# Mamba's opening split in two: the first four tiles' step sizes and splits are made in the FFN block ahead, the other twelve tiles' follow

## The chip, the core and the metric

The kernel runs on one NeuronCore of a Trainium2 chip. A core has a matrix engine (TensorE, PE in the profile; its weight loads are shown as PEld), a vector engine (VectorE, DVE), an activation engine (ScalarE, ACT), a general engine (GpSimd, POOL) and a queue that issues transfers (SyncE, SP). Each engine works through its own list of instructions in order; semaphores make one wait for another. Matrix results land in PSUM banks, everything else lies in SBUF. The metric is the time of one execution in microseconds (us); lower is better. The time before is 738.0 us, the median of 3 runs (737.44 to 738.93).

## What is computed

Six stages run over 8 sequences of 256 tokens with 128 channels, which are 16 tiles of 128 tokens: a mixture-of-experts FFN, an RWKV block, the same FFN again, a second kind of FFN, a Mamba-2 block, and the second FFN again. The change lies at the seam between the fourth stage and the fifth. Of the Mamba block this matters (N is 16 heads, chunks have 64 tokens):

```python
def mamba2_forward(x, W_in, W_dt, b_dt, W_B, W_C, W_out, A_log):
    xz = x @ W_in.T
    x_in, z = (xz[..., :d], xz[..., d:])
    dt = jax.nn.softplus(x @ W_dt.T + b_dt)
    A = -jnp.exp(A_log)[None, None, :] * dt
    B = (x @ W_B.T).reshape(b, L, h, n)
    C = (x @ W_C.T).reshape(b, L, h, n)
    X = x_in.reshape(b, L, h, p) * dt[..., None]
    Y, new_state = ssd_minimal(X, A, B, C, CHUNK)   # decays exp(cumulated A)
    y = Y.reshape(b, L, d) * jax.nn.silu(z)
    return (y @ W_out.T, new_state)
```

`dt` are the step sizes and `A` the decays, 16 numbers for each token; the decays have to be cumulated along the tokens before the chunks can be worked on.

## The kernel before, in words

**The FFN stream.** `ffn_stream` works in blocks of 4 tiles (512 tokens). The two FFN stages ahead of Mamba are one stream of 8 blocks; the last, block 7, has 12 units p = 0 to 11, two shared ones, eight experts, two shared ones. The order is written out by hand: at unit p, PE makes the two up projections of unit p + 4 (into `ps_a`, `ps_b`, 6 matmuls of 512 columns) and the down projection of unit p (`ps_acc`, 3 matmuls); ACT takes the SiLU of unit p + 4 and rounds unit p + 2 (`hhi`); DVE multiplies for unit p + 4 (`gated`) and takes the remainder of unit p + 2 (`hlo`); POOL weighs the experts. Since a product of 32-bit numbers is made of three passes over rounded and remaining parts (`three_pass`, L98 to L100), nearly every operand has a `hi` and a `lo`.

**What the stream already does for Mamba.** With `heads` set it also normalises and turns the first 12 tiles of Mamba's input: `measure` (L508, L512), POOL's `scale`, `normal` (L520, writes `norm_xn`), `turn_x` (L269, PE transposes into `ps_t`), `high_x` (L389) and `low_x` (L527). Block 10 of this count, which is tiles 8 to 11, is the last: in block 7 DVE normalises it at p = 8, PE turns it at p = 9, ahead of the down projections 10 and 11, ACT and DVE split it at p = 10. Then come `take_out` (L411), `turn_out` (L311) and `add_out` (L559), and a barrier of all engines.

**The opening of `mamba_phase`.** On PE: `steps(0, 12)` (36 matmuls, each with 16 moving columns and 128 columns of weights, tile by tile against `w["dt"]`, into `mb_pyt`), `project(0)` and `project(1)` (input projections, 6 matmuls of 256 columns for two tiles, into the two banks `mb_c`), `turn` (L1864, tiles 12 to 15, which are normalised only here), `project(2)`, `project(3)`, `steps(12, 16)`, `project(4)` to `project(7)`, `cumulate(0)` (L1800: 8 matmuls against the triangle `le` for tiles 0 to 3), `begin_piece(0)`, the sums over all decays (L1907), `begin_piece(1)` to `(3)` (B and C of sequence 0, 12 matmuls of 256 columns each), then the sections. A section is one sequence: four groups of heads, each with decays (L1768), products of B and C (L1793), outputs (L1816) and a piece of the next sequence's B and C.

On ACT: the projections' copies `take_in(k)` (L1975, L1976, which free the bank for `project(k + 2)`), softplus of all 16 tiles at once (Exp L1993, Ln L1995), `take_sums(0)` (L1984), Exp of the sums (`ee`, L2001), the copies `take_bc` (L1929). Exp and Ln need different function tables, so an `ACT_TABLE_LOAD` stands between them.

On DVE: the statistics of the last four tiles, five masks from the identity (`row_masks`, L2027 to L2032), `normed` (L2162), `low_x` (L2168), the triangles' rounded copies (L2178 to L2180), then one chain over 16 tiles (128x256): bias and `-|u|` (L2182, L2185), `dt` (L2187), `dA` (L2189), the split of dA on a grid (`split_sums`, L2038 to L2047: `grid`, `cut`, `cuthi`, `cutlo`), the first four tiles widened to 128 columns (L2049, L2052), the decays' hi and lo (L2191, L2193), `row_parts(0)` (L2063, L2069, L2070), the other twelve tiles' widening (L2057). POOL makes the norm's factors, clears `xp` and `xd`, makes the triangles, and then the first sequence's ranges and inputs.

## Time and profile before

| what | value |
|---|---|
| median of 3 runs | 738.0 us (737.44 to 738.93) |
| the profiled execution | 742.08 us, its span 740.0 us |
| PE busy in the span | 688.9 us (93%) |
| DVE, ACT, POOL busy | 567.0, 415.2, 321.4 us (77%, 56%, 43%) |
| last FFN block's first seam rows to the barrier | 414.9 to 421.7 us |
| Mamba's opening on PE | 421.7 to 454.4 us |
| Mamba's sections on PE | 454.4 to about 618 us |

The span runs from the first instruction to the last of one profiled execution, 2.1 us shorter than that execution's own time and itself 4.1 us over the median of the unprofiled runs. Timeline rows give the start in us from the span's beginning, the length, the engine, the line of the kernel, the operation, what is written from what, and in brackets how long the engine had been idle and who released it. Matmuls are pipelined: their lengths overlap, so the distance between starts is what one costs. The granted clock of TensorE is given as a share of full speed: 1.00 is its 2.4 GHz level, 0.50 its 1.2 GHz level.

### The profile page before, as it was taken

How to read it: one execution, taken by the hardware profiler on the slowest of the kernel's cores; microseconds unless marked ns; L12 is line 12 of the kernel's file. 1: busy time of each engine (PE TensorE's matmuls, PEld its weight loads, DVE VectorE, ACT ScalarE, POOL GpSimd, SP SyncE). 2: the span in 40 equal slices, each digit the busy share in tenths (PEclk: the TensorE clock that was granted, in tenths of full speed). 3: DMA queues.
4: the chain of work that ended last, by engine and by line, in shares of the span. 5: the costliest groups of instructions: out<-in, count | busy, mean ns of one | idle time of the engine just before them, and what ended most of it. 6: DMA issues, size and time to landing. Idle time of an engine off the chain costs nothing. (4 is left out here: it accounts for less than half of the span.)

```text
span 740.0 us, 12506 instructions
## 1 busy us (share of the span) xinstructions
PE 688.9 (93%) x4132; PEld 517.6 (70%) x4132; DVE 567.0 (77%) x1293; ACT 415.2 (56%) x751; POOL 321.4 (43%) x404
## 2 busy tenths in 40 slices
PE   6899989697879999999999778999999997999997
PEld 5677764543457777777778677777777775777785
DVE  5788987899968878987989734566666674889774
ACT  4556775885235555556656446565555553555553
POOL 2658872201217766465668315211413200546463
PEclk9999998999999999999999879999999998999999
DMA  6636510000004232222223000000000000323141
GB/s 169 192 104 181 169 57 1 0 1 1 1 30 143 71 103 96 78 66 80 85 67 106 1 0 1 2 1 2 2 1 1 0 1 1 103 71 121 54 125 43
DMA packets 34329, 43.16 MB, mean 58 GB/s; under 512 B 5216, under 2 KB 17504, under 8 KB 34272
## 3 DMA queue, kind: packets, MB, share of 16 engines
q1 hardware_dynamic: 34272, 42.46, 18.5%
q8 instruction: 29, 0.48, 0.3%
q14 instruction: 28, 0.23, 0.1%
HBM read 41.13 MB, written 1.31 MB: 57 GB/s over the span
## 5 line engine op out<-in xcount | busy, mean ns | idle before, releaser
L677 POOL TENSOR_TENSOR p_prod<-p_p,p_gate_row 128x512 f32<-128x512 f32 x128 | 201.9, 1588 | 110.8 <-DVE p_p L494 64.2
L376 ACT ACTIVATE p_sil<-p_ps_a 128x512 f32<-128x512 f32 x176 | 105.1, 597 | 133.7 <-PE p_ps_a L100 130.2
L499 DVE TENSOR_TENSOR p_hlo<-p_prod,p_hhi 128x512 fp32r<-128x512 f32 x176 | 149.8, 853 | 0.3 <-ACT p_hhi L385 0.2
L494 DVE TENSOR_TENSOR p_p<-p_sil,p_ps_b 128x512 f32<-128x512 f32 x128 | 87.2, 681 | 53.1 <-ACT p_sil L376 39.6
L385 ACT CAST p_hhi<-p_prod 128x512 fp32r<-128x512 f32 x176 | 107.8, 614 | 22.5 <-POOL p_prod L677 22.3
L98 PE MATMUL p_ps_a<-xt_hi,w_uphi 128*128 128x512 f32 x176 | 74.7, 424 | 0.0
L98 PE MATMUL p_ps_acc<-p_hhi,w_downhi 128*128 128x512 f32 x176 | 72.2, 410 | 2.6 <-DVE p_hlo L499 2.5
L98 PE MATMUL p_ps_b<-xt_hi,w_uphi 128*128 128x512 f32 x176 | 71.3, 405 | 1.1 <-DVE p_prod L494 1.1
L100 PE MATMUL p_ps_b<-xt_hi,w_uplo 128*128 128x512 f32 x176 | 70.7, 402 | 0.0
L100 PE MATMUL p_ps_a<-xt_hi,w_uplo 128*128 128x512 f32 x176 | 70.4, 400 | 0.0
L99 PE MATMUL p_ps_acc<-p_hlo,w_downhi 128*128 128x512 f32 x176 | 70.4, 400 | 0.0
L100 PE MATMUL p_ps_acc<-p_hhi,w_downlo 128*128 128x512 f32 x176 | 70.3, 400 | 0.0
L99 PE MATMUL p_ps_a<-xt_lo,w_uphi 128*128 128x512 f32 x176 | 70.2, 399 | 0.0
L99 PE MATMUL p_ps_b<-xt_lo,w_uphi 128*128 128x512 f32 x176 | 70.2, 399 | 0.0
L2078 DVE TENSOR_TENSOR mb_sm<-mb_sm,mb_c 128x512 f32<-128x512 f32 x64 | 43.7, 687 | 27.3 <-ACT mb_off L1951 21.4
L1793 PE MATMUL mb_c<-mb_bc 64*128 64x128 f32 (+1 forms) x512 | 58.9, 349 | 1.3 <-ACT mb_bc L1929 1.3
L1929 ACT COPY mb_bc<-mb_c 128x1024 f32<-128x1024 f32 x32 | 32.4, 1013 | 45.8 <-PE mb_c L100 45.8
L2085 DVE SCALAR_TENSOR_TENSOR mb_sm<-mb_d,mb_later 128x512 f32<-128x512 f32 x64 | 41.2, 685 | 20.7 <-PE mb_d L1768 20.5
L1793 PEld LDWEIGHTS mb_c<-mb_bc 64*128 64x128 f32 x512 | 38.9, 186 | 20.7 <-issue 16.0
L1948 ACT ACTIVATE mb_sm<-mb_sm 128x512 f32<-128x512 f32 x64 | 40.4, 632 | 16.9 <-DVE mb_sm L2085 16.1
L2233 POOL TENSOR_TENSOR w_downhi<-mb_widehi,mb_own 128x512 fp32r<-128x512 f32 x8 | 9.0, 1129 | 94.1 <-DVE norm_moments L2104 46.9
L98 PEld LDWEIGHTS p_ps_b<-xt_hi,w_uphi 128*128 128x128 f32 x176 | 33.5, 190 | 12.1 <-DVE p_p L494 2.3
(345 smaller groups left out, 1452.9 us busy)
## 6 DMA issues: line engine op xcount, KB each, us to landing
p_gate_row<-gate_rows SPq DMA_DIRECT2D x128, 256.0 KB, 3.3
w_rawbuf<-in_L_ffn_fc_w_dram SPq DMA_DIRECT2D x3, 512.0 KB, 6.5
w_rawbuf<-in_L_ffn_w_dram SPq DMA_DIRECT2D x3, 512.0 KB, 6.3
out_dram<-x SPq DMA_DIRECT2D x4, 256.0 KB, 3.7
w_rawbuf<-in_L_ffn_shared_w_dram SPq DMA_DIRECT2D x3, 256.0 KB, 5.7
x<-in_L_attn_x_dram SPq DMA_DIRECT2D x2, 256.0 KB, 3.7
x<-in_L_attn_x_dram SPq DMA_DIRECT2D x1, 512.0 KB, 8.8
mb_xraw<-in_L_attn_W_B_dram SPq DMA_DIRECT2D x1, 512.0 KB, 4.5
```

Of the source, the lines that this page charges most:

```text
L98: pe.matmul(out, weights[0], moving[0], start=start, stop=False)
L99: pe.matmul(out, weights[0], moving[1], start=False, stop=False)
L100: return pe.matmul(out, weights[1], moving[0], start=False, stop=stop)
L376: nc.scalar.activation(sil[:, u % 2], ps_a[:, u % 2], ACT.Silu).then_inc(c["sil"].sem, 1)
L385: nc.scalar.copy(hhi[:, u % R], prod[:, u % R]).then_inc(c["hhi"].sem, 1)
L494: nc.vector.tensor_tensor(dst, sil[:, u % 2], ps_b[:, u % 2], ALU.mult).then_inc(c["p1"].sem, 1)
L499: nc.vector.tensor_tensor(hlo[:, u % R], prod[:, u % R], hhi[:, u % R].bitcast(F32), ALU.subtract).then_inc(c["hlo"].sem, 1)
L677: G.tensor_tensor(prod[:, u % R], p1[:, u % 2], gate_row[:, e % ROWS], ALU.mult).then_inc(c["prod"].sem, 1)
L1793: last = pe.matmul(half(q, t, more)[:, k, 0:SEQ - t * P], bc[h][state, r, j, bass.ts(t, P)], bc[h][state, 2 + r, j, t * P:SEQ], start=True ...
L1948: A(sm[q % 2][t][:], sm[q % 2][t][:], ACT.Exp).then_inc(c["m_E"].sem, 1)
L2078: V.tensor_tensor(sm[q % 2][t][:], sm[q % 2][t][:], half(q, t, more)[:, :, 0:P], ALU.mult).then_inc(c["m_read"].sem, 1)
L2085: V.scalar_tensor_tensor(out=sm[q % 2][t][:], in0=ps_d[t][:], scalar=0.0, in1=later[:].unsqueeze(1).broadcast_to([P, 4, P]), op0=ALU.min, ...
```

## The change

A new class `MambaHead` holds the step sizes' tiles and work, in parts: part 0 is tiles 0 to 3 (the first two sequences), part 1 the other twelve. Part 0 is done inside FFN block 7:

- PE, after down projection 1: `steps` for four tiles, 12 matmuls into the idle logits bank `ps_l`.
- DVE: the triangles' copies in block 6 at p = 9; `biased` at p = 3, `row_masks` at p = 7, `step_sizes` and `split_sums` at p = 10 of block 7.
- ACT at p = 9: Exp of `a_log` and of part 0, a table load ahead of them, a second table load and Ln.
- POOL in block 6 at p = 8: the triangles.

In Mamba's opening PE begins with `project(0)`, `project(1)`, then `cumulate(0)`, `turn`, `project(2)`, `project(3)`, all `steps` of tiles 4 to 15 (36 matmuls), the sums of the first two sequences, `project(4)` to `project(7)`, and four pieces in a row. DVE widens, splits and makes `row_parts(0)` before `low_x`; the chain of part 1 (128x192) follows. ACT takes the sums' Exp in three parts. The sums of the other six sequences, the widening of the twelve tiles and the copies for them move into the first section; `cumulate(1)` with its copy and `row_parts(1)` move from that section's second group of heads to its fourth.

The names with `mb_` in the rows below are the tiles named above; `mb_stage` holds `u` and then `dt`, `mb_na` first `-|u|` and then `dA`. Semaphores (`r_...`) keep the names of an earlier stage.

DVE in block 7, from p = 7 on, before:

```order
L494 TENSOR_TENSOR p_prod<-p_sil,p_ps_b 128x512 [waits s_hhi,s_hlo,s_b,s_sil]
L499 TENSOR_TENSOR p_hlo<-p_prod,p_hhi 128x512 [waits s_hhi] x2
L527 TENSOR_TENSOR xt_lo<-p_ps_t,xt_hi 128x512 [waits s_xhi]
L520 SCALAR_TENSOR_TENSOR norm_xn<-x,norm_moments,norm_rstd 128x128 [waits s_xt,s_rstd,s_moments]
L520 SCALAR_TENSOR_TENSOR norm_xn<-x,norm_moments,norm_rstd 128x128 x3
L499 TENSOR_TENSOR p_hlo<-p_prod,p_hhi 128x512 [waits s_hhi]
```
and now:

```order
L505 TENSOR_TENSOR p_prod<-p_sil,p_ps_b 128x512 [waits s_hhi,s_hlo,s_b,s_sil]
L510 TENSOR_TENSOR p_hlo<-p_prod,p_hhi 128x512 [waits s_hhi]
L1709 TENSOR_REDUCE mb_odd<-ident 128x1
L1710 TENSOR_REDUCE mb_even<-ident 128x1
L1711 TENSOR_REDUCE mb_minus_odd<-ident 128x1
L1712 TENSOR_REDUCE mb_minus_low<-ident 128x1
L1714 TENSOR_REDUCE mb_own<-ident 128x4
L510 TENSOR_TENSOR p_hlo<-p_prod,p_hhi 128x512 [waits s_hhi]
L538 TENSOR_TENSOR xt_lo<-p_ps_t,xt_hi 128x512 [waits s_xhi]
L531 SCALAR_TENSOR_TENSOR norm_xn<-x,norm_moments,norm_rstd 128x128 [waits s_xt,s_rstd,s_moments]
```
Five reductions (the masks) now stand between two remainders of block 7, ahead of `norm_xn`, on which PE's turn waits.

DVE at the end of block 7, before:

```order
L499 TENSOR_TENSOR p_hlo<-p_prod,p_hhi 128x512 [waits s_hhi]
L527 TENSOR_TENSOR xt_lo<-p_ps_t,xt_hi 128x512 [waits s_xhi]
L559 SCALAR_TENSOR_TENSOR x<-p_ps_o,x 128x512 [waits s_ot]
L190 UNCONDITIONAL_BRANCH
L2020 UNCONDITIONAL_BRANCH [waits barrier_Pool_Activation_PE_DVE_SP_release]
```
and now:

```order
L510 TENSOR_TENSOR p_hlo<-p_prod,p_hhi 128x512 [waits s_hhi]
L538 TENSOR_TENSOR xt_lo<-p_ps_t,xt_hi 128x512 [waits s_xhi]
L1662 SCALAR_TENSOR_TENSOR mb_stage<-mb_stage,mb_na 128x64 [waits r_ln]
L1664 SCALAR_TENSOR_TENSOR mb_na<-mb_stage,mb_expa 128x64 [waits r_g2]
L1675 TENSOR_SCALAR mb_grid<-mb_na 128x64 [waits r_low2]
L1677 TENSOR_SCALAR mb_cut<-mb_grid 128x64 [waits r_p]
L1679 SCALAR_TENSOR_TENSOR mb_cut<-mb_na,mb_cut 128x64 [waits r_p]
L1682 CAST mb_cuthi<-mb_cut 128x2x64 [waits r_p]
L1684 TENSOR_TENSOR mb_cutlo<-mb_cut,mb_cuthi 128x2x64 [waits r_x2]
L570 SCALAR_TENSOR_TENSOR x<-p_ps_o,x 128x512 [waits s_ot]
L190 UNCONDITIONAL_BRANCH
```
Seven dependent operations on the first four tiles now stand between `low_x` and the block's `add_out`.

ACT in the opening around softplus, before (after the copies of `project(3)`):

```order
L1993 ACTIVATE mb_na<-mb_na 128x256 [waits r_d]
L1995 ACT_TABLE_LOAD
L1995 ACTIVATE mb_na<-mb_na 128x256 [waits r_S]
L1975 COPY mb_xraw<-mb_c 128x256 [waits r_g]
L1976 ACTIVATE mb_zs<-mb_c 128x256
```
and now (from the same point):

```order
L2107 ACT_TABLE_LOAD
L2107 ACTIVATE mb_ee<-mb_y 128x2x16 [waits r_ev]
L2094 COPY mb_xraw<-mb_c 128x256 [waits r_g]
L2095 ACTIVATE mb_zs<-mb_c 128x256
L2094 COPY mb_xraw<-mb_c 128x256 [waits r_g]
L2095 ACTIVATE mb_zs<-mb_c 128x256
L1654 ACTIVATE mb_na<-mb_na 128x192 [waits r_d]
L1656 ACT_TABLE_LOAD
L1656 ACTIVATE mb_na<-mb_na 128x192 [waits r_S]
```
The Exp of the first sums, with its table load, now stands ahead of the copies of projections 4 and 5, softplus behind them; the copies of 6 and 7, another table load and Exp, and the four B and C copies follow.

The diff, cut to its core:

```diff
 ffn_stream, PE
+                    if heads and (n, p) == (BLOCKS - 1, 1):
+                        pe.wait_ge(c["lgs"].sem, c["lgs"].at(BLOCKS))
+                        pe.wait_ge(c["xlo"].sem, c["xlo"].at(BLOCKS + 1))
+                        pe.wait_ge(c["raw_lo"].sem, c["raw_lo"].at(2))
+                        heads.steps(pe, 0, BT, by_tile(ps_l))
 ffn_stream, ACT
+                    if heads and (n, p) == (BLOCKS - 1, 9):
+                        heads.softplus(act, 0, 0, BT)
 ffn_stream, DVE
+                        if p == 3:
+                            dve.wait_ge(c["raw_lo"].sem, c["raw_lo"].at(len(splits)))
+                            heads.biased(dve, 0, 0, BT, by_tile(ps_l))
+                        if p == 7:
+                            heads.row_masks(dve)
                         if p == 10:
                             low_x(BLOCKS + 2)
+                            heads.step_sizes(dve, 0, 0, BT)
+                            heads.split_sums(dve, 0, 0, BT)
+                    if heads and (n, p) == (BLOCKS - 2, 9):
+                        heads.masks(dve)
 ffn_stream, POOL
+                    if heads and (n, p) == (BLOCKS - 2, 8):
+                        heads.triangles(pool)
 MambaHead
+    def softplus(self, act, part, a, b):
+        act.wait_ge(c["m_na"].sem, c["m_na"].at(part + 1))
+        if part == 0:
+            A(self.exp_a[:], self.vec["a_log"][:], ACT.Exp)
+        A(some, some, ACT.Exp).then_inc(c["m_ex"].sem, 1)
+        act.wait_ge(c["m_ex"].sem, c["m_ex"].at(part + 1))
+        A(some, some, ACT.Ln, bias=1.0).then_inc(c["m_ln"].sem, 1)
...
 mamba_phase, PE
-            steps(0, 3 * BT)
             project(0)
             project(1)
+            pe.wait_ge(c["m_first"].sem, c["m_first"].at(1))
+            cumulate(0, sums_of[0])
             turn()
             project(2)
             project(3)
             pe.wait_ge(c["m_xl"].sem, c["m_xl"].at(1))
-            steps(3 * BT, TILES).then_inc(c["m_pu"].sem, 1)
+            head.steps(pe, BT, TILES, ps_u)
+            sums(0, 0, 2)
             for k in range(4, 8):
                 project(k)
-            pe.wait_ge(c["m_first"].sem, c["m_first"].at(1))
-            cumulate(0, sums_of[0])
-            begin_piece(0)
-            pe.wait_ge(c["m_dl"].sem, c["m_dl"].at(1))
...
-            begin_piece(1)
-            begin_piece(2)
-            begin_piece(3)
+            for k in range(4):
+                begin_piece(k)
 mamba_phase, ACT
             take_in(0)
             take_in(1)
+            take_sums(0)
             take_x()
             take_in(2)
             take_in(3)
...
+            take_ends(0, 0, 1)
+            take_in(4)
+            take_in(5)
+            head.softplus(act, 1, BT, TILES)
+            take_in(6)
+            take_in(7)
+            take_ends(0, 1, 2)
+            for k in range(4):
+                take_bc(0, 0, k, ps_c[k % 2])
 mamba_phase, DVE
             measured_last()
-            row_masks()
+            widen_first()
             normed()
+            split_decays(0, 0, BT)
+            row_parts(0, sums_of[0])
             low_x()
...
+            head.biased(dve, 1, BT, TILES, ps_u)
+            head.step_sizes(dve, 1, BT, TILES)
+            head.split_sums(dve, 1, BT, TILES)
+            split_decays(1, BT, TILES)
```

## Rows read from the trace of the kernel before

**Rows 1.** Engines by stretch: busy us, instructions, granted clock share (PEclk), DMA.

```profile
core 0: us, PE busy (x) PEld busy (x) DVE busy (x) ACT busy (x) POOL busy (x), PEclk, DMA share, GB/s
400.00:414.90 14.90, 14.73 (x66) 11.63 (x65) 14.07 (x28) 8.49 (x16) 11.26 (x9) 1.00 0.14 47
414.90:421.70 6.80, 3.17 (x16) 1.89 (x16) 4.28 (x13) 1.82 (x3) 0.00 (x0) 1.00 0.00 0
421.70:429.40 7.70, 7.68 (x37) 7.70 (x37) 2.60 (x16) 0.85 (x2) 4.87 (x10) 0.50 0.01 3
429.40:435.40 6.00, 6.00 (x29) 6.00 (x30) 1.10 (x4) 2.56 (x7) 0.00 (x0) 0.50 0.00 0
435.50:436.70 1.20, 1.20 (x13) 1.20 (x13) 0.00 (x0) 0.66 (x2) 0.00 (x0) 1.00 0.00 0
435.40:445.50 10.10, 6.12 (x50) 5.71 (x50) 5.27 (x15) 5.50 (x14) 0.00 (x0) 1.00 0.00 0
445.50:449.00 3.50, 3.50 (x19) 3.50 (x18) 2.69 (x5) 1.90 (x3) 1.32 (x1) 0.52 0.02 5
449.20:452.80 3.60, 3.60 (x31) 3.51 (x30) 0.00 (x0) 3.58 (x6) 3.52 (x13) 1.00 0.00 0
474.50:600.00 125.50, 124.43 (x1377) 94.45 (x1376) 84.74 (x169) 72.55 (x118) 29.08 (x91) 1.00 0.01 1
```

**Rows 2.** Timeline, DVE, last FFN block: start, length, operation, idle before, releaser.

```profile
406.17 0.69 DVE L494 TENSOR_TENSOR p_p<-p_sil,p_ps_b 128x512 f32<-128x512 f32 x1 [0.59 <-PE p_ps_b L100]
...
413.65 1.29 DVE L499 TENSOR_TENSOR p_hlo<-p_prod,p_hhi 128x512 fp32r<-128x512 f32 x2
...
417.95 0.69 DVE L527 TENSOR_TENSOR xt_lo<-p_ps_t,xt_hi 128x512 fp32r<-128x512 f32 x1 [0.77 <-ACT xt_hi L389]
...
420.08 0.69 DVE L559 SCALAR_TENSOR_TENSOR x<-p_ps_o,x 128x512 f32<-128x512 f32 x1 [1.43 <-PE p_ps_o L311]
```

**Rows 3.** Timeline, PE and ACT, from the last FFN block's end into the opening.

```profile
416.64 0.66 PE L269 MATMUL p_ps_t<-ident,norm_xn 128*128 128x128 f32 x4 [1.29 <-DVE norm_xn L520]
417.34 0.59 ACT L389 CAST xt_hi<-p_ps_t 128x512 fp32r<-128x512 f32 x1 [2.69 <-PE p_ps_t L269]
...
421.72 0.35 PE L98 MATMUL mb_pyt<-w_uphi,xt_hi 128*128 128x16 f32 x1 [1.68 <-PEq L190]
```

**Rows 4.** Timeline, PE, the opening: the turn, a wait for ACT, the first products.

```profile
432.10 1.05 PE L1864 MATMUL mb_y<-ident,mb_sm 128*128 128x128 f32 x4
...
440.55 0.39 PE L98 MATMUL mb_c<-w_uphi,xt_hi 128*128 128x256 f32 x1 [2.19 <-ACT mb_zs L1976]
...
454.43 1.58 PE L1793 MATMUL mb_c<-mb_bc 64*128 64x256 f32 x16 [0.85 <-ACT mb_bc L1929]
```

**Rows 5.** Timeline, DVE, the opening: the five masks, first and last.

```profile
422.29 0.18 DVE L2027 TENSOR_REDUCE mb_odd<-ident 128x1 f32<-128x64 f32 x1
...
422.77 0.37 DVE L2032 TENSOR_REDUCE mb_own<-ident 128x4 f32<-128x128 f32 x1
```

**Rows 6.** Timeline, ACT and DVE, the first sums' copy and the row parts.

```profile
445.19 0.59 ACT L1984 CAST mb_off<-mb_d 128x512 fp32r<-128x512 f32 x1 [2.24 <-PE mb_d L1800]
445.81 0.75 DVE L2063 SCALAR_TENSOR_TENSOR mb_parts<-mb_off,mb_minus_low,mb_d 128x512 fp32r<-128x512 f32 x1 [1.16 <-ACT mb_off L1984]
447.06 0.54 DVE L2070 TENSOR_SCALAR mb_widelo<-mb_parts,mb_minus_odd,mb_even 128x512 fp32r<-128x512 f32 x1
```

**Rows 7.** Timeline, ACT, the opening: softplus, table loads, copies.

```profile
438.24 1.28 ACT L1995 ACT_TABLE_LOAD   x1
439.54 0.42 ACT L1995 ACTIVATE mb_na<-mb_na 128x256 f32<-128x256 f32 x1
439.86 0.35 ACT L1975 COPY mb_xraw<-mb_c 128x256 f32<-128x256 f32 x1
...
440.64 0.41 ACT L1976 ACTIVATE mb_zs<-mb_c 128x256 f32<-128x256 f32 x1
...
447.36 1.01 ACT L1929 COPY mb_bc<-mb_c 128x1024 f32<-128x1024 f32 x1 [1.58 <-PE mb_c L100]
```

More of the change, by code:

```diff
@@ L108, in __init__, with ffn_stream @@
         self.units, self.shared = weights.units, weights.shared
-def ffn_stream(nc, tag, counts, spare, sb, ps, x, xt, consts, kinds, gate_dram, norm, loads=(), splits=(), out_dram=None, entry=None, begun=0, tail=None, heads=False, opening=None):
+def ffn_stream(nc, tag, counts, spare, sb, ps, x, xt, consts, kinds, gate_dram, norm, loads=(), splits=(), out_dram=None, entry=None, begun=0, tail=None, heads=None, opening=None):
     splits = split_jobs(splits)
@@ L1799, in cumulate @@
                     for k in range(2):
-                        last = pe.matmul(bank[:, t], wide[k][:, g * BT + t], consts["le"][:], start=k == 0, stop=k == 1)
+                        last = pe.matmul(bank[:, t], wide[k][:, g * BT + t], head.le[:], start=k == 0, stop=k == 1)
                 last.then_inc(c["m_C"].sem, 1)
@@ L1865, in turn, with sums @@
                 last.then_inc(c["m_t"].sem, 1)
-            def steps(a, b):
-                for t in range(a, b):
-                    last = three_pass(pe, ps_u[:, t], [q[:, bass.ts(t, P)] for q in xt], w["dt"], True, True)
-                return last
+            def sums(part, a, b):
+                pe.wait_ge(c["m_dl"].sem, c["m_dl"].at(part + 1))
+                for t, tri in ((0, head.gt), (1, head.le)):
+                    for k in range(2):
+                        some = dAp[k][:].rearrange("p (m t) h -> p t m h", t=2)[:, t, a:b]
+                        last = pe.matmul(ps_sum[:, t, a:b], tri[:], some, start=k == 0, stop=k == 1)
+                last.then_inc(c["m_sum"].sem, 1)
             def project(k):
```

235 lines of the change are left out of this document (128 added, 107 removed).

## The prediction

> **What bounds the kernel now.** I read the table of engines by stretch first. In the FFN block ahead of the seam PE is busy 14.73 of 14.9 us, in the sections behind it 124.43 of 125.5 us [rows 1]: there only PE's work counts. Between the two lie 6.8 us of the block's tail, with PE busy 3.17, and the opening. I count the opening from PE's first matmul at 421.72 [rows 3] to the first products of B and C at 454.43 [rows 4], 32.7 us; behind that point the old list and the new one hold nearly the same work. What the change is worth is this length, plus what it adds ahead of the barrier.
>
> Three things are to be seen in the opening. First, the 36 step matmuls take all of 421.7 to 429.4, at a granted clock of 0.50, the 1.2 GHz level (7.7 us over 36, 0.213 each), before any projection starts. Secondly, the clock comes up to 2.4 GHz only at 435.4, after 6.0 us of projections and a turn; then a step matmul costs 0.11 us (1.2 us; of 13 counted two are cut off at the edges) and one of 256 columns 0.12 (3.6 us, 31 counted) [rows 1]. Thirdly, PE stands still for copies that are queued behind softplus on ACT (2.19 us before 440.55, rows 4), and it falls to 0.52 once more for 3.5 us at 445.5 [rows 1].
>
> **The FFN block ahead (dearer).** PE gets 12 step matmuls at p = 1. It runs at 1.00 without a gap there, so they cost 12 x 0.11 = 1.3 us. The logits bank, the turned tiles and `w["dt"]` are ready long before. DVE waited 0.59 us for PE at 406.17 [rows 2], so it moves along by the whole 1.3; the two small operations of `biased` fit into that wait.
>
> The five masks at p = 7 run from 422.29 to 423.14 in the opening today, 0.85 us [rows 5]. In their new place DVE has no idle time until `norm_xn`, and PE waits 1.29 us for just that [rows 2, 3]: +0.85.
>
> Behind `low_x` come seven dependent operations of 64 to 128 columns. Five masks in 0.85 us, and 0.18 for one of 64 columns, bound one at 0.17 to 0.37 with its wait [rows 5]; I take 0.25, near the small one plus a semaphore, so 1.75 us (1.2 to 2.6). They start 1.3 + 0.85 later than `low_x` ends today (418.64), at 420.8, and end at 422.5; `add_out` would come at 420.08 + 2.15 = 422.23 [rows 2]. So +0.3 (0 to 1.1).
>
> ACT's softplus of part 0 costs two table loads of 1.28 us and three small functions (0.42 for 256 columns, so 0.2 to 0.4 each), 3.3 us [rows 7]. ACT is free from 414.65 + 1.3 and is needed for the turned block at 417.34 + 2.15 = 419.49, with 3.5 us between [rows 3]. It hides with 0.2 us to spare; if it doesn't fit, up to 0.5 us falls on the tail. The four triangle operations on POOL and their three copies on DVE (three of the masks' size, 0.5) lie in block 6, ahead of DVE's next wait for PE, and POOL has idle time (11.26 of 14.9 us busy, rows 1): nothing; without that cover 0.5.
>
> Sum ahead of the barrier: 1.3 + 0.85 + 0.3 = **+2.5 us** (2.2 to 3.9).
>
> **The opening (cheaper).** Let t be the time since PE's first matmul. At the 1.2 GHz level: projections 0 and 1, 12 x 0.213 = 2.6; `cumulate(0)`, 8 x 0.213 = 1.7 (its operands are ready at t = 1.5); `turn`, 0.7 (of its 1.05 in rows 4 the last part overlaps what follows); projections 2 and 3 from t = 5.1. The clock came up 6.0 us after the first projection [rows 1]; taken over, they end at 7.0. Meanwhile ACT copies the first sums (0.59), DVE makes `row_parts(0)` (445.81 to 447.60, 1.8 us [rows 6]) and then `low_x` (0.69 [rows 2]): 4.5 + 0.6 + 1.8 + 0.7 = 7.6, so PE waits 0.6 us for it. The 36 step matmuls then cost 36 x 0.11 = 4.0 at 2.4 GHz: done at S = 11.6.
>
> From S on ACT sets the pace. Sums 0.5; table load and small Exp 1.5; two `take_in` 1.2 (439.86 to 441.05, rows 7); softplus 0.4 + 1.3 + 0.4 = 2.1; two `take_in` 1.2; table load and Exp 1.5; four copies of B and C, 1.0 each [rows 7]. The third and the fourth wait for pieces, 12 x 0.12 = 1.45 us each, which wait for the banks: piece 2 starts at S + 9.1, piece 3 ends at S + 12.1, its copy at S + 13.1. DVE's chain for part 1 (nine operations of 192 columns, some 3.5 us) runs beside this and is done before the first section needs it. So the products start at t = 24.8 if the clock stays up.
>
> It will hardly stay up. The long row of 16-column matmuls is just what ran at 1.2 GHz for 7.7 us without bringing the clock up, and a wait of 2.19 us before 440.55 was followed, 5 us later, by 3.5 us at 0.52 [rows 1, 4]. One such stretch costs 3.5 / 2 = 1.7 us of PE's work, of which ACT hides a little: +1.5. That makes t = 26.4 against 32.7: **-6.3 us** (-8 to -4).
>
> **The first section.** `row_parts(1)`, 1.8 us, moves from its second group of heads to the fourth, just ahead of the next section's first operations on DVE, where a second `row_parts` follows. PE may miss 0.3 us (0 to 0.6). The widening copies fall into ACT's and DVE's waits for PE, which has the most to do there (124.4 us of 125.5 against 72.6 and 84.7, rows 1).
>
> **Sum.** 2.5 - 6.3 + 0.3 = -3.5 us. On the profiled execution, 742.1 becomes 738.6; that one lies 4.1 above the median of the runs, and the same difference on 738.0 gives **734.5 us**.
>
> **A rule of the Trainium skill** speaks against the change. The trace shows a table load of 1.28 us at 438.24 and the Ln at 439.54, 0.02 us behind it [rows 7]. "ScalarE: Activation LUTs", section "What ACT_TABLE_LOAD costs", gives about 1.28 us for the load and another 1.38 for a drain, 2.66 in all for each switch. The load agrees; the row leaves no room for the drain. By the page the three loads in the new chain would add 4.1 us of drains, and the sum would be +0.6.
>
> **The rivals.**
> - *The clock does not come up before the steps.* The 128-column matmuls of `cumulate(0)` now stand among the projections, and nothing in the rows says that such a mixture raises the clock in 6 us. Then projections 2 and 3 end at 7.7, the 36 steps cost 7.7 as today, S = 15.3, and with the next two projections slow as well (+1.0) the products start at 29.4: -3.3 + 2.8 = -0.5, **737.5 us**. For it: the first 13.7 us of today's opening are at 0.50. Against it: the projections there did raise it.
> - *Slower: the clock stays down until the sections.* The new list gives PE a wait at every second step (`low_x`, the copies, the banks), and waits came ahead of each fall. S = 15.3; with the pieces at 0.213 (12 x 0.09 = 1.1 more each, of which 1.6 us show in all) the products start at 31; and the first section's matmuls run slow for a stretch like that of 3.5 us, +1.7. 31 + 1.7 = 32.7, nothing is gained, and the 2.8 us ahead of the barrier and in the section stay: **740.8 us**. It decides from the point where the opening is longer than 32.7 - 2.8 = 29.9. Against it: at 445.5 back-to-back pieces brought the clock back in 3.5 us.
> - *Table switches cost twice their load.* If ACT stood still for as long again as each of the three loads in its chain (3 x 1.28), -3.5 becomes +0.3, **738.3 us**. The 0.02 us behind the load speaks against it. By the skill's page, above, it would be +0.6.
> - *Part 0 shortens nothing*, since the long chain of part 1 takes its place and ACT ends as late as before. It would need S + 13.1 = 32.7, S = 19.6, and is contained in the slower case.
>
> **How the numbers follow.** The forecast has 0.56 (it needs the clock to rise within some 8 us of the opening), the first rival 0.26, the slower one 0.14, the table rival 0.04. A measurement of this kernel can tell about 0.2% from no change, 1.5 us. Most of the forecast's own range (-5.8 to -1.2) is below that line, a small part not; the first rival reaches from -1.9 to +0.8. That gives faster 0.57, within 0.2% 0.30, slower 0.13. The range for 8 in 10 goes from 732.0 (an opening of 24.7 with 2.2 ahead of it) to 739.5, inside the slower case.
>
> **What would show it.** Right: the last FFN block's turn of `norm_xn` comes 2.1 to 2.2 us later, the barrier about 2.5; the opening's 36 steps take near 4 us and stand at 1.00 for most of it; the first products come about 26 us after the first projection. The wait of 2.2 us for `mb_zs` and the one ahead of `cumulate(0)` are gone, and PE waits for ACT's copies around the table loads. Wrong: steps at 0.213 each (first rival); a granted clock of 0.5 also under the pieces (slower); more than 0.1 us between a table load and its function; or a tail of the FFN block that grows by more than 4 us.

## The result

The changed kernel takes 735.5 us (median, 733.0 to 741.2) against 738.7 for the kernel before beside it (736.2 to 742.8); the ratio is 0.9957, 95% interval 0.9938 to 0.9975. A second comparison of the same two kernels, in a later set of runs, gave 736.9 against 738.7, ratio 0.9968 (0.9951 to 0.9986). So it is faster by 0.3 to 0.4%, 2 to 3 us. The profiled execution has a span of 739.2 us against 740.0; it happens to be a long one, for two reasons that come below.

Medians and ratios rest on 12 executions of most of the kernels below (16 in the first comparison), but on 10 of e2, e5 and e8, 8 of e6, 7 of e4 and only 4 of e12, and since executions more than 1.5% above a kernel's fastest count as disturbed, which may leave out real ones where the clock of TensorE decides, a ratio from few executions describes those and not the kernel.

**The opening after.** Engines by stretch, the changed kernel, cut where the granted clock changes (columns as in [rows 1]): the last FFN block, its tail, then four stretches from the opening's start to the first products, and the sections.

```profile
402.20:417.10 14.90, 14.89 (x73) 12.09 (x71) 12.77 (x28) 7.59 (x15) 11.87 (x10) 1.00 0.15 53
417.10:427.60 10.50, 5.88 (x20) 3.88 (x21) 8.15 (x26) 5.46 (x9) 0.74 (x2) 0.84 0.01 2
427.50:431.00 3.50, 3.38 (x16) 3.42 (x17) 2.47 (x14) 1.10 (x4) 2.00 (x3) 0.51 0.00 0
431.00:437.75 6.75, 5.52 (x49) 5.32 (x49) 2.87 (x7) 3.89 (x8) 4.27 (x6) 1.00 0.00 0
437.75:444.75 7.00, 7.00 (x35) 7.00 (x35) 0.71 (x2) 2.11 (x7) 3.66 (x14) 0.51 0.00 0
444.75:453.90 9.15, 7.49 (x58) 6.67 (x57) 3.70 (x11) 7.83 (x12) 3.91 (x14) 1.00 0.01 2
474.50:600.00 125.50, 124.44 (x1379) 94.76 (x1379) 85.41 (x171) 72.17 (x118) 31.49 (x94) 1.00 0.01 1
```

Timeline of PE: the tail's turn and last transposes, the opening's first matmul, the first and the last of the 36 steps, the first of the sums, the wait ahead of the second piece, the first products.

```profile
421.25 1.11 PE L273 MATMUL p_ps_t<-ident,norm_xn 128*128 128x128 f32 x4 [2.09 <-DVE norm_xn L531]
...
425.31 0.66 PE L315 MATMUL p_ps_o<-ident,p_acc_s 128*128 128x128 f32 x4 [0.68 <-ACT p_acc_s L420]
427.62 0.55 PE L98 MATMUL mb_c<-w_uphi,xt_hi 128*128 128x256 f32 x1 [1.65 <-PEq L190]
...
434.74 0.28 PE L98 MATMUL mb_pyt<-w_uphi,xt_hi 128*128 128x16 f32 x1 [1.23 <-DVE xt_lo L2274]
...
439.47 0.36 PE L100 MATMUL mb_pyt<-w_uphi,xt_lo 128*128 128x16 f32 x1
439.68 0.37 PE L1993 MATMUL mb_y<-mb_dAhi,mb_gt 128*128 128x32 f32 x1
...
446.66 0.39 PE L98 MATMUL mb_c<-xt_hi,w_uphi 128*128 128x256 f32 x1 [1.22 <-ACT mb_zs L2095]
...
453.88 1.58 PE L1910 MATMUL mb_c<-mb_bc 64*128 64x256 f32 x16 [0.44 <-ACT mb_bc L2044]
```

From the first matmul at 427.62 to the first products at 453.88 are 26.26 us, where [rows 3, 4] have 32.71. Of the signs that the prediction named, the wait ahead of `cumulate(0)` is gone; the wait for `mb_zs`, 2.19 us in [rows 4], is not gone but 1.22 and in another place; the steps run from 434.74 to 439.68, 4.9 us, the first 27 of the 36 at 1.00; behind the copies PE waits for ACT (0.44). The clock is 0.51 twice in the opening, for 3.4 and 6.8 us (the stretches above are cut at quarters of a us).

ACT in the opening, from the third projection's copy on:

```profile
434.22 1.28 ACT L2107 ACT_TABLE_LOAD   x1
440.73 0.20 ACT L2107 ACTIVATE mb_ee<-mb_y 128x32 f32<-128x32 f32 x1 [5.23 <-PE mb_y L1993]
442.20 0.37 ACT L2094 COPY mb_xraw<-mb_c 128x256 f32<-128x256 f32 x1 [1.27 <-PE mb_c L100]
...
444.02 0.36 ACT L1654 ACTIVATE mb_na<-mb_na 128x192 f32<-128x192 f32 x1
444.41 1.28 ACT L1656 ACT_TABLE_LOAD   x1
445.70 0.36 ACT L1656 ACTIVATE mb_na<-mb_na 128x192 f32<-128x192 f32 x1
...
447.18 1.28 ACT L2107 ACT_TABLE_LOAD   x1
448.47 0.20 ACT L2107 ACTIVATE mb_ee<-mb_y 128x32 f32<-128x32 f32 x1
448.57 1.01 ACT L2044 COPY mb_bc<-mb_c 128x1024 f32<-128x1024 f32 x1
```

Every load takes 1.28 us. Where its function has its input, it starts 0.01 us behind the load. The first load is issued at once, while its function waits 5.23 us for PE: it costs nothing. In these rows a load stands at every change between Exp and Ln; whether one table could serve both was not tried.

**The FFN block's tail after.** DVE's first and last mask, `norm_xn`, the first and the last of the seven operations on part 0, and `add_out`:

```profile
418.07 0.21 DVE L1709 TENSOR_REDUCE mb_odd<-ident 128x1 f32<-128x64 f32 x1
...
418.57 0.37 DVE L1714 TENSOR_REDUCE mb_own<-ident 128x4 f32<-128x128 f32 x1
...
420.06 1.14 DVE L531 SCALAR_TENSOR_TENSOR norm_xn<-x,norm_moments,norm_rstd 128x128 f32<-128x128 f32 x4
...
423.63 0.21 DVE L1662 SCALAR_TENSOR_TENSOR mb_stage<-mb_stage,mb_na 128x64 f32<-128x64 f32 x1
...
425.11 0.29 DVE L1684 TENSOR_TENSOR mb_cutlo<-mb_cut,mb_cuthi 128x128 fp32r<-128x128 f32 x1
426.00 0.69 DVE L570 SCALAR_TENSOR_TENSOR x<-p_ps_o,x 128x512 f32<-128x512 f32 x1 [0.60 <-PE p_ps_o L315]
```

For comparisons I use lengths between fixed points of PE's timeline: **block 7** is the distance from the last transposes (`turn_out`) of block 6 to those of block 7; the **opening** is the distance from PE's first matmul there to the first products; **the seam** is from `turn_out` of block 6 to the first products, with the barrier in it. They don't depend on how a run starts, which the spans do: the first `turn_out` of the whole program comes at 48.96 us before and 51.46 after, and this offset of 2.5 us hides most of the gain in the two spans.

| kernel | block 7 | opening | seam | clock at 0.50 or 0.51 in the opening, lengths of the stretches |
|---|---|---|---|---|
| before | 22.30 | 32.71 | 57.35 | 13.7, 3.4 |
| changed | 26.09 | 26.26 | 54.66 | 3.4, 6.8 |
| changed, second profile (e9) | 24.74 | 25.98 | 53.36 | 3.4, 6.8 |
| e1 steps in block 7 | 23.64 | 33.81 | 59.75 | 13.3, 6.8 |
| e2 masks early | 24.07 | 26.67 | 53.58 | 10.2 |
| e3 steps first | 24.74 | 25.78 | 53.01 | 6.8, 3.4 |
| e4 filled waits | 24.74 | 25.11 | 52.34 | 6.8 |
| e5 one Exp | 26.31 | 28.87 | 57.49 | 3.4, 6.8, 3.4 |
| e6 steps twice | 24.76 | 33.64 | 60.89 | 6.8, 13.7 |
| e7 all three | 24.08 | 28.03 | 54.93 | 10.2 |
| e8 part 0 late | 24.50 | 28.98 | 56.24 | 8.6, 6.8 |
| e10 steps spread | 25.94 | 28.67 | 57.06 | 20.5 |
| e11 masks early, filled | 24.07 | 26.84 | 53.58 | 10.2 |
| e12 e11 and steps spread | 24.03 | 20.67 | 47.53 | none |

Behind the first products all kernels are alike: from there to the last `turn_out` they take 280.4 to 281.5 us, 281.46 before and 281.20 after.

### The profile page after: what moved, and what is told of

It reads as the page before. It is cut to its first block and busy times, and to the rows that moved or that the text cites. A ratio compares the mean times of both kernels' runs of the same rounds, so it can differ in the third digit from the quotient of the medians.

```text
span 739.2 us, 12530 instructions
## 1 busy us (share of the span) xinstructions
PE 689.3 (93%) x4136; PEld 516.8 (70%) x4136; DVE 568.1 (77%) x1303; ACT 419.2 (57%) x757; POOL 322.2 (44%) x404
## 5 line engine op out<-in xcount | busy, mean ns | idle before, releaser
L394 ACT CAST p_hhi<-p_prod 128x512 fp32r<-128x512 f32 x176 | 108.0, 615 | 23.3 <-POOL p_prod L697 23.2
L2063 ACT ACTIVATE mb_sm<-mb_sm 128x512 f32<-128x512 f32 x64 | 40.4, 632 | 17.1 <-DVE mb_sm L2189 16.0
L98 PEld LDWEIGHTS p_ps_acc<-p_hhi,w_downhi 128*128 128x128 f32 x176 | 33.9, 192 | 12.0 <-DVE p_hlo L510 4.6
```

The source lines that it names most:

```text
L98: pe.matmul(out, weights[0], moving[0], start=start, stop=False)
L394: nc.scalar.copy(hhi[:, u % R], prod[:, u % R]).then_inc(c["hhi"].sem, 1)
L2063: A(sm[q % 2][t][:], sm[q % 2][t][:], ACT.Exp).then_inc(c["m_E"].sem, 1)
```

## The experiments

### Steps alone in the FFN block (e1)

```diff
 before, ffn_stream, PE, after down projection 1 of block 7
+    for t in range(BT):
+        three_pass(pe, bank[:, t], ..., heads, True, True)
```

> The kernel before, with 12 step matmuls (128x16) added in FFN block 7 behind down projection 1, their result read by nobody; the opening does all its work as before. Theory (PE bounds the block there, so its added matmuls are paid in full): from the turn_out of block 6 to that of block 7 on PE 22.3 us becomes 23.6; the opening stays at 32.7 but for the clock; the time is 1.3 us over that of the kernel before (ratio 1.0018). Rival (the longer block in the changed kernel comes from what DVE and ACT got, and PE has slack): 22.3 us and ratio 1.000.

Block 7 goes from 22.30 to 23.64, +1.34, which is 12 matmuls at 0.11, with nothing hidden. The opening is 1.1 longer; its second stretch at 0.51 lasted 6.8 us in this profile instead of 3.4, which can account for it. The median is 741.2, ratio 1.0016 (0.9992 to 1.0040).

### The masks moved ahead (e2)

```diff
 changed kernel, ffn_stream, DVE, block 7
+    if p == 2:
+        heads.row_masks(dve)
     if p == 3:
         ...
-    if p == 7:
-        heads.row_masks(dve)
```

> The changed kernel with the five masks at p = 2 of block 7, where DVE waits 1.5 us for PE, instead of p = 7. Theory (at p = 7 they stand on the way to norm_xn): block 7 on PE falls from 26.1 us by 0.85, and by up to 1.2 more if TensorE's clock then stays at 2.4 GHz through the tail; opening as it is (26.3); ratio to the kernel before 0.9957 becomes 0.993 to 0.9945. Rival (the masks fitted into slack, the tail is long for another reason): block 7 stays at 26 us, ratio 0.9957.

Block 7 is 24.07, against 24.74 for the masks at p = 7 where the clock is 1.00 throughout (e3, e4, e9), 0.67 less. This is a difference between two places, not the masks' whole cost at p = 7, which is 0.80: at p = 2, too, they delay DVE a little (the block's first `norm_xn` comes 0.1 later than in e9). And 0.2 to 0.3 of the 0.67 comes back behind block 7, where the distance from the last transposes to the opening is 2.83 us instead of 2.49 (e3, e4) to 2.64 (e9). PE's wait ahead of the turn falls from 2.09 to 1.28:

```profile
415.15 0.66 PE L273 MATMUL p_ps_t<-ident,norm_xn 128*128 128x128 f32 x4 [1.28 <-DVE norm_xn L531]
```

The ratio to before is 0.9954 (0.9921 to 0.9987), which can't be told from the changed kernel's; its centre misses the 0.993 to 0.9945 expected. In this profile the clock stayed at 1.00 up to 8.9 us into the opening, but then was 0.51 for 10.2 us, and the opening was no shorter (26.67).

### Steps of tiles 4 to 11 at the head of the opening (e3)

```diff
 changed kernel, mamba_phase, PE
+    for t in range(BT, 3 * BT):
+        three_pass(pe, ps_u[:, t], ..., w["dt"], True, True)
     project(0)
     ...
-    head.steps(pe, BT, TILES, ps_u)
+    head.steps(pe, 3 * BT, TILES, ps_u)
```

> The changed kernel with the step matmuls of tiles 4 to 11 (24 of the 36) put back ahead of project(0); part 0 stays in the FFN block. Theory (the opening's gain is that PE no longer spends its first us on step matmuls at 1.2 GHz, while ACT and DVE wait): +5.1 us ahead of the first projection, 3 us less behind project(3), so the opening goes from 26.3 to 28 to 29.5 us and the ratio to 0.998 to 1.000. Rival (the gain is that part 0's chain is off the path, wherever the steps stand): opening 26.3, ratio 0.9957.

The opening takes 25.78 us, 0.5 less than the changed kernel's, although 24 of the steps run first and at 0.51. The ratio is 0.9956 (0.9934 to 0.9978), that of the changed kernel. So my theory that the new order of the steps carries the gain falls. That the gain comes instead from part 0's chain being off the path, so that its sums and then ACT's list can start early, fits this run, but e3 doesn't show it by itself.

### Matmuls of no use in PE's waits of the tail (e4)

```diff
 changed kernel, ffn_stream, PE, block 7
+    fill(5)     # 512 columns each, result not read
     turn_x(BLOCKS + 2)
     ...
     turn_out(...)
+    fill(4)
```

> The changed kernel with matmuls of 512 columns that nobody reads in two of PE's waits: five ahead of the last turn of norm_xn in block 7 and four behind the last turn_out, ahead of the barrier. Theory (1.2 us of the tail's 3.8 us of growth and the slow first projections are the clock, which falls because PE idles there): granted clock 1.00 through block 7's tail and into the opening, block 7 25.0 us instead of 26.1, opening 24.5 to 25.5 instead of 26.3, ratio 0.992 to 0.9945. Rival (the clock falls anyway, or the added matmuls delay PE): block 7 at 26 us or above, ratio 0.9957 or above.

Block 7 is 24.74, just as without the filler, so the five matmuls lie wholly in the wait. The clock is 1.00 through the tail and for the first 10.6 us of the opening, and the opening takes 25.11. The ratio is 0.9937 (0.9906 to 0.9968), of seven executions; its interval overlaps the changed kernel's.

### One Exp for the ends (e5)

```diff
 changed kernel, mamba_phase, ACT
-    take_ends(0, 0, 1)
     take_in(4)
     take_in(5)
     head.softplus(act, 1, BT, TILES)
     take_in(6)
     take_in(7)
-    take_ends(0, 1, 2)
+    take_ends(0, 0, 2)
```

> The changed kernel, but the Exp of the sums of the first two sequences is made once, behind take_in(7), instead of in two parts, the first ahead of take_in(4). Nothing is left out; ACT's list in the opening has one table load less. Theory (a table load costs ACT its 1.28 us and no more, and the one ahead of the first sums' Exp lies in ACT's wait for PE): what is taken away was hidden up to the Exp's own 0.2 us, while the load that softplus now needs comes behind the copies of projections 4 and 5, on ACT's path. The distance from PE's first matmul of the opening to the first products stays within -0.3 and +1.3 us of 26.3. Rival (each switch of tables costs the load and as much again, wherever it stands): the distance shrinks by 1.5 to 2.8 us.

It is slower: 738.3 us, ratio to before 1.0006 (0.9989 to 1.0023), so the whole gain is lost. The opening takes 28.87. ACT:

```profile
438.35 0.39 ACT L2095 ACTIVATE mb_zs<-mb_c 128x256 f32<-128x256 f32 x1
438.75 1.28 ACT L1654 ACT_TABLE_LOAD   x1
440.05 0.36 ACT L1654 ACTIVATE mb_na<-mb_na 128x192 f32<-128x192 f32 x1
440.43 1.28 ACT L1656 ACT_TABLE_LOAD   x1
441.72 0.36 ACT L1656 ACTIVATE mb_na<-mb_na 128x192 f32<-128x192 f32 x1
...
443.20 1.28 ACT L2107 ACT_TABLE_LOAD   x1
```

and PE behind it:

```profile
442.68 0.39 PE L98 MATMUL mb_c<-xt_hi,w_uphi 128*128 128x256 f32 x1 [2.42 <-ACT mb_zs L2095]
```

I had expected one load less in ACT's list. There is none less: the opening has three loads in either kernel (434.22, 444.41 and 447.18 in the changed one, 438.75, 440.43 and 443.20 here), since the function ahead of the opening is the Ln of part 0 and the next Exp needs its table again. What changed is the place of the first. With the small Exp ahead, the table of Exp was loaded in ACT's long wait for the sums; without it the load comes behind the copies, where nothing hides it, and PE's wait for `mb_zs` grows from 1.22 to 2.42, nearly by the 1.28 of one load. I had given this up to +1.3, and measured were +2.6. The clock fell again 0.4 us after that wait, for 3.4 us, beneath the pieces (their distance 0.21 instead of 0.12), and this can be the rest. For the rival, that each switch costs double, the run is no test, since it has as many switches; what speaks against it is the 0.01 us behind each load.

### The opening's steps twice (e6)

```diff
 changed kernel, mamba_phase, PE
+    for t in range(BT, TILES):
+        three_pass(pe, ps_u[:, t], ..., w["dt"], True, True)
     head.steps(pe, BT, TILES, ps_u)
```

> The changed kernel with the 36 step matmuls of the opening issued twice, the second time over the same bank; nothing is left out. Theory (the steps stand on the path and from their end S on ACT sets the pace): S comes later by the 36 matmuls at the clock of that place, 4.0 us at 1.00 and up to 7.7 at 0.50, and the first products come later by the same amount, less at most 0.5. Rival (from the projections on ACT's copies and tables set the length whatever PE does before): the products come less than 2 us later.

The products come 33.64 us after the first matmul, 7.4 later than in the changed kernel, and the last step ends 7.4 later (19.24 against 11.85 for its start). The median is 742.7; the ratio rises from 0.9957 to 1.0061, by 7.7 us. So the end of the steps, S, carries over one to one, and nothing that ACT has queued hides it. The rival (less than 2 us) falls. The stretches show what the clock did:

```profile
426.75:430.00 3.25, 3.25 (x32) 3.25 (x30) 0.00 (x0) 1.94 (x3) 1.52 (x3) 1.00 0.00 0
430.00:443.75 13.75, 13.75 (x66) 13.75 (x66) 0.72 (x2) 2.08 (x7) 3.64 (x14) 0.51 0.00 1
```

The row of narrow matmuls began at 426.61 at full clock; 3.5 us later the clock fell, under a PE that had no gap, and it stayed down for the rest of the steps and until 4 us of projections had passed. The 13.75 us show 13.75 busy.

### All three together (e7), and with the second Exp again (e11)

```diff
 changed kernel
+    masks at p = 2 as in e2, fill(5) and fill(4) as in e4
 e7 only
-    take_ends(0, 0, 1), take_ends(0, 1, 2)
+    take_ends(0, 0, 2) as in e5
```

> The changed kernel with the masks at p = 2, the filler matmuls in PE's two waits of block 7's tail (five of 512 columns ahead of the last turn, four behind the last turn_out, results not read), and one Exp for the ends of the first two sequences. Nothing is left out. Theory (the masks at p = 7 cost 0.7 us, the clock stays up through the tail, the table load is hidden): block 7 takes 24.1 us, the opening 25 to 26, from turn_out of block 6 to the first products 51.6 to 52.6 us where the changed kernel's profile had 54.7; the median lies 0.5 to 1.5 us below the changed kernel's, 734.0 to 735.0. Rival (the clock falls at other places instead, so the time gets back what the tail gained): no nearer than 0.3 us to a gain over the changed kernel.

> The changed kernel with the masks at p = 2 and the filler matmuls in PE's two waits of block 7's tail, and with the Exp of the ends in two parts again, as the changed kernel has it. Nothing is left out. Theory (the one Exp cost the combination of the run before 2 to 3 us): block 7 24.1 us, opening 25.1 to 26.0, from turn_out of block 6 to the first products 51.7 to 52.6, and a median 1 to 2 us below the changed kernel's beside it. Rival (the masks and the filler together bring a fall of the clock elsewhere, and the one Exp was not to blame): 54 us or more, and no gain.

With one Exp it is 737.2 us, ratio 0.9987 (0.9962 to 1.0012): block 7 as expected (24.08), the opening 28.03. With the Exp in two parts it is 734.3, ratio 0.9952 (0.9934 to 0.9971), opening 26.84. So the one Exp costs 2.6 us by the ratios (1.2 in the openings of the two profiles), as it cost e5 its gain, and my theory for e7, that the load was hidden and one could be saved, was wrong. The opening of e11 is above the 25.1 to 26.0 expected: its clock held into the steps and then fell for 10.2 us instead of 6.8. In the same set the changed kernel had 736.9; e11's centre is 0.16% lower, but the intervals overlap, so a gain over the changed kernel is not shown.

### Part 0's work back in the opening (e8)

```diff
 changed kernel, ffn_stream
-    heads.steps, heads.biased, heads.softplus, heads.step_sizes, heads.split_sums of part 0
 mamba_phase, PE
+    head.steps(pe, 0, BT, ps_u)
     project(0)
     project(1)
-    cumulate(0)
     turn()
     project(2)
     project(3)
+    cumulate(0)
 mamba_phase, ACT and DVE
+    softplus of part 0 at the head of ACT's list, take_sums(0) behind take_in(3)
+    bias, step sizes and splits at the head of DVE's, low_x ahead of row_parts(0)
```

> The changed kernel with part 0's work put back into the opening: its 12 step matmuls first on PE, then projections 0 to 3 around the turn, cumulate(0) behind project(3); its bias, softplus, step sizes and splits at the head of DVE's and ACT's lists there. Masks and triangles stay in the FFN block. Nothing is left out. It separates doing part 0 ahead of the barrier from splitting the chain in two. Theory (the work ahead of the barrier is what pays): block 7 shrinks to 23.2 us (24.7 less 1.3 and 0.3), and the opening grows by 12 steps at 0.50 (2.6) and a wait of about 1 us for part 0's chain ahead of cumulate(0), to 29.5 to 30.5; from turn_out of block 6 to the first products 55.2 to 56.2 us, 2 above the changed kernel where its clock stays up (53.0). Rival (the split of the chain is what pays, the place of part 0 doesn't matter): the distance is within 0.7 us of 53.0.

The ratio is 0.9984 (0.9961 to 1.0007) and the seam 56.24 us, 2.9 above the changed kernel's second profile and at the upper end of what the theory gave; the clock fell in the tail of this profile, which made the last three down projections 0.6 us and the transposes 0.4 us longer. Block 7 took 24.50 where 23.2 was expected; with 0.6 for the clock, 0.7 are left, and they are a delay of DVE: the block's first `norm_xn` starts 11.06 us behind block 6's `turn_out`, 10.31 in the kernel before. The likely cause is the triangles' copies, which lengthen DVE's list in block 6; without the steps, DVE waits for PE only once ahead of that `norm_xn` and doesn't make it up. The opening took 28.98, half a microsecond less than the theory's least: part 0's chain was done before PE asked for it.

Against the kernel before, splitting the chain alone gives 1.1 us of the seam in this pair of profiles, and doing part 0 ahead of the barrier another 2.9. But this pair doesn't separate the place of part 0 from the course of the clock: from the turn to the first products the clock was down for 20.5 us in e8 and 10.2 in e9, and 10 us more at half the clock are worth up to 5 us of PE's work, more than the whole 2.9. By the ratios the two parts are 1.2 and 1.2 to 2.0 us, and the intervals leave both of them open. So which part of the change carries the gain is not shown by this run.

### The changed kernel again (e9), and its steps spread (e10)

```diff
 changed kernel, mamba_phase, PE (e10)
     project(0)
+    some_steps(4, 6)
     project(1)
     cumulate(0, sums_of[0])
+    some_steps(6, 8)
     turn()
+    some_steps(8, 10)
     project(2)
+    some_steps(10, 12)
     project(3)
-    head.steps(pe, BT, TILES, ps_u)
+    head.steps(pe, 3 * BT, TILES, ps_u)
```

> The changed kernel once more, unedited, as the yardstick for the three runs beside it. The kernel before and this one: ratio 0.9957 within its interval of 0.9938 to 0.9975. In the profile: block 7 takes 24.7 us if the clock stays up through its tail, 26.1 if it falls there; the opening 25.5 to 26.5 us.

> The changed kernel with the step matmuls of tiles 4 to 11 spread over the opening, six at a time (two tiles) between projections 0 to 3, cumulate(0) and the turn; only the last twelve stay where all 36 stood. Nothing is left out. In six profiles so far the granted clock fell 2.1 to 3.4 us after the row of 16-column matmuls had begun and stayed down for about 7 us. Theory (the row itself brings the clock down): with no row longer than twelve the fall inside the steps does not come, and the opening takes 24.0 to 25.3 us; the median falls 0.7 to 1.5 us below the changed kernel's. Rival (the clock falls for another reason, the waits around it or the time since its last rise): a stretch of 7 us at 0.50 is there as before and the opening takes 25.5 us or more.

e9 is unedited: 736.9 us, ratio 0.9968 (0.9951 to 0.9986). Its profile has block 7 at 24.74, without a fall of the clock in the tail; the first profile had 26.09 with one. The same program does either.

e10 is slower than e9 by 0.34%: 739.3 us, ratio to before 1.0002 (0.9987 to 1.0018). The theory falls in this form. Its stretches:

```profile
422.25:425.50 3.25, 1.44 (x10) 1.24 (x11) 2.20 (x11) 0.00 (x0) 1.11 (x2) 1.00 0.02 5
425.50:446.25 20.75, 20.09 (x97) 19.80 (x95) 5.73 (x17) 9.17 (x22) 10.72 (x23) 0.51 0.00 0
```

The clock fell 0.9 us into the opening; in every kernel with these waits in the tail it was down by then. Among projections with steps between them it didn't come up again for 20.5 us. In the changed kernel it came back after 3.4 us of projections and `cumulate(0)` without steps (6.8 us in e6).

### Masks early, waits filled, steps spread (e12)

> The kernel of masks at p = 2 and filler matmuls, with the steps spread as in the run with the spread alone. Nothing is left out. Theory: both gains add up, block 7 24.1 us and opening 24.0 to 25.3, from turn_out of block 6 to the first products 50.6 to 51.9, median 1.5 to 3 us below the changed kernel's. Rival (the clock's falls only change places): the same as the better of the two alone.

The edit is e11's and e10's together.

```profile
412.89:416.89 4.00, 3.69 (x17) 2.82 (x18) 3.06 (x9) 3.85 (x7) 0.00 (x0) 1.00 0.01 2
...
420.90:428.90 8.00, 8.00 (x71) 8.00 (x72) 5.38 (x19) 4.07 (x11) 5.81 (x8) 1.00 0.01 2
428.90:441.50 12.60, 10.68 (x81) 9.66 (x80) 5.36 (x12) 10.96 (x19) 8.57 (x29) 1.00 0.00 1
```

The clock stays at 1.00 through the tail (first row: from 8 to 4 us ahead of the opening PE is busy 3.69 of 4.00 us) and the whole opening, which takes 20.67 us with all its 36 steps; the seam is 47.53 us, 9.8 below before. Its four executions have a median of 728.8 us (727.6 to 729.9), ratio 0.9870 (0.9855 to 0.9886). The theory had 24.0 to 25.3 for this opening and a median 1.5 to 3 us below the changed kernel's; it is 8.1 below. How often this kernel runs so is open, and it may be seldom: the median is of four executions where the kernels beside it have twelve, and any above 738.5 us, 1.5% over the fastest, would be missing from it, while e10 takes 739.3 with the clock down. If all eight are missing for that reason, most executions are no faster than the kernel before. So 728.8 is shown as what it can do, not as its typical time. The four are of one kind: their mean granted clock over the whole execution is 0.987 to 0.993, in e10's twelve it is 0.970 to 0.977. The two kernels share the opening and differ only in the tail: in these executions the spread helps where the clock is up when the opening starts, and harms where it is down.

### The clock over all profiles

Fourteen profiles give this. In the nine with PE's tail as the changed kernel or the kernel before have it (before, changed, e1, e3, e5, e6, e8, e9, e10) the masks came late or not at all and nothing filled PE's waits; in each the clock was down within 1 us of the opening's start, in four of them (changed, e5, e8, e10) already in the tail. In the five with the masks early or the waits filled (e2, e4, e7, e11, e12) it was 1.00 at that point. The length of the wait ahead of the turn alone doesn't separate them: 1.29 us before and 1.28 in e2. What does is open for e2, which has one profile; for the masks without filler matmuls this profile is all there is, the other four have them. What came next was the steps: where all 36 stood in a row at full clock, the clock fell 2.2 to 3.9 us after the row began (changed, e2, e4 to e9, e11; 434.74 and 437.8 in the changed kernel). In the changed kernel PE had waited 1.23 us just before, but in e6 3.5 us of the row passed without a gap. Where they were spread and the clock was up, it did not fall. That narrow matmuls bring the clock down is so supported by e6 and by e12 against e11, which differ in their order alone; e12's profile is one, but its four executions have a mean clock of 0.987 to 0.993, e11's twelve 0.976 to 0.987.

"TensorE: Matmul & The Clock Gate" of the Trainium skill, Part 1, ties the clock to how busy PE has been. The trace agrees in kind for the waits of the tail, where a fall comes behind idle time. It does not for the steps: PE shows 7.00 of 7.00 us busy at 0.51 in the changed kernel and 13.75 of 13.75 in e6. The busy time of the profile is not the activity that the clock goes by.

## Why the prediction was right

It said 734.5 us, -3.5; measured were -3.2 (first comparison) and -1.8 (second). Term by term, on the two profiles:

- **What bounds.** Right: behind the first products nothing moved (281.46 and 281.20 us), and all of the difference lies in block 7 and the opening.
- **12 steps, +1.3.** Right, e1 shows +1.34.
- **Masks, +0.85.** Right: DVE has no idle time around them, and they put off what follows by 0.80 (416.74 to 417.54 below). The 0.67 of e2 is smaller because the masks aren't free at p = 2 either.
- **The two operations of `biased`, nothing.** Wrong, 0.3. They were to fit into DVE's wait for PE. In their place e1, which has the steps and not them, waits 0.81 us; they take 1.25 (407.44 to 408.69), the second 1.07 alone, and the next product starts without idle time, 0.3 later than in e1 when counted from block 6's `turn_out`. DVE in e9:

```profile
406.24 0.69 DVE L505 TENSOR_TENSOR p_p<-p_sil,p_ps_b 128x512 f32<-128x512 f32 x1 [0.59 <-PE p_ps_b L100]
...
407.44 0.22 DVE L1642 TENSOR_TENSOR mb_stage<-p_ps_l,mb_bdt 128x64 f32<-128x64 f32 x1
407.70 1.07 DVE L1645 SCALAR_TENSOR_TENSOR mb_na<-mb_stage 128x64 f32<-128x64 f32 x1
408.69 0.68 DVE L505 TENSOR_TENSOR p_p<-p_sil,p_ps_b 128x512 f32<-128x512 f32 x1
...
416.74 0.21 DVE L1709 TENSOR_REDUCE mb_odd<-ident 128x1 f32<-128x64 f32 x1
...
417.54 0.68 DVE L510 TENSOR_TENSOR p_hlo<-p_prod,p_hhi 128x512 fp32r<-128x512 f32 x1
```

- **Triangles in block 6, nothing.** Right in this kernel, where the steps give DVE waits that cover them; e8, without the steps, shows a delay of 0.7 that is likely theirs.
- **Seven operations, +0.3 (0 to 1.1).** Right where the clock stays up. They stand 0.25 apart, as taken. In the second profile (e9) `add_out` follows the last of them without idle time, 2.30 us behind `low_x`'s start instead of 2.13 [rows 2]; from the last transposes to the opening it is 2.64 us (2.49 in e3, e4 and e6) against 2.34. So they cost 0.15 to 0.3 (0.3 to 0.5 where the masks stand early, with 2.68 to 2.83). In the first profile PE was slower than they, and `add_out` waited 0.60 us for it (fence above). DVE in e9:

```profile
421.23 0.69 DVE L538 TENSOR_TENSOR xt_lo<-p_ps_t,xt_hi 128x512 fp32r<-128x512 f32 x1 [0.77 <-ACT xt_hi L398]
...
423.32 0.29 DVE L1684 TENSOR_TENSOR mb_cutlo<-mb_cut,mb_cuthi 128x128 fp32r<-128x128 f32 x1
423.53 0.68 DVE L570 SCALAR_TENSOR_TENSOR x<-p_ps_o,x 128x512 f32<-128x512 f32 x1
```

- **Softplus of part 0, hidden with 0.2 us.** Hidden: in e9 `xt_hi` still waits 0.49 us for PE's turn behind the Ln. In e2, e7, e11 and e12, where the turn is earlier, it follows the Ln without idle time, so the cover ends there.
- **Sum ahead of the barrier, +2.5 (2.2 to 3.9).** Block 7 is 2.44 longer where the clock stays up (24.74 against 22.30; e3, e4, e9), which is 1.34 for the steps, 0.3 for `biased` and 0.8 for the masks, and with the 0.15 to 0.3 above it makes 2.6 to 2.7. That this lies 0.1 to 0.2 from the sum hides the missing term of 0.3; and the upper bound of 3.9 is less than the terms' own upper ends give (1.3, 0.85, 1.1 and twice 0.5, 4.25). In the first profile block 7 was 3.79 longer: the clock fell 0.5 us ahead of the turn (four transposes 1.11 us, [rows 3] 0.66; down projections behind them at 0.43 instead of 0.23). That the longer wait for `norm_xn`, 1.29 to 2.09, could bring the clock down was not among the terms. With a wait of 2.1 us the clock fell in block 7's tail in four of seven profiles (changed, e5, e8, e10; not e3, e6, e9), with 1.3 us in none of three (before, e1, e2); it costs 1.35 us in the changed kernel's first profile.
- **The opening, -6.3.** -6.45 and -6.7. S, the end of the steps, was put at 11.6 and came at 12.1 and 11.8. From S to the products were foreseen 13.2 and +1.5 for a slow stretch; it took 14.2. (Its own parts, 11.6 + 13.1 + 1.5, make 26.2 and not 26.4, a slip of 0.2.) But two errors hide in this. The small Exp was taken to cost a load (1.5 us); the load was hidden, so it cost 0.2. And the clock took another course: it came up after 3.4 us instead of 6 to 7, and then fell under the steps for 6.8 us instead of 3.5 under the pieces. The sum of both stretches, 10.2 us, was about what I had assumed; that is luck. Before, the clock was down for 17.1 us of the opening, so up to 3.4 us of the gain can be the clock's course and not the shorter chain; no run separates the two.
- **First section, +0.3.** Not seen; from the products on the changed kernel is 0.26 us shorter, inside the 1.1 us by which this length differs between kernels.
- **Rivals.** That the clock doesn't come up before the steps did not happen in the changed kernel; e10, where it stays down for 20.5 us, takes 739.3 us. The slower case did not come either; its condition was an opening over 29.9. Double cost of table switches: out. Of the changed kernel's five loads at the seam four have their function 0.01 us behind, and the fifth's waits for PE; over the fourteen profiles it is 196 of 248 loads. The figure of 1.38 us for a drain in "ScalarE: Activation LUTs" of the Trainium skill, section "What ACT_TABLE_LOAD costs", shows nowhere in this kernel.

What the prediction had right in method was that one list after another was followed with its own waits. What it lacked was a term for the operations of `biased`, and any for what its new wait in the tail does to the clock.

## What to carry to other kernels

When a chain is split and its first part moved ahead, add up what each moved step costs in its new place against the engine that sets the end there: here 2.7 us were paid for 6.6. A table load that can be issued into a wait is free; take away the small function behind it, and the next function of that table pays for the load, so ask of each load where it stands and not only how many there are. Where PE has many matmuls of few columns, try them between wide ones and keep PE busy ahead of them (20.67 us for the opening in e12, one profile); if the clock is already down when they start, this order can keep it down (e10, 20.5 us).
